# A four-layer network over eight batches on one core: normalized inputs made one stage earlier, a reciprocal spread over 64 rows, and new hand-written orders

## The reference

```python
x = x + _layernorm(_L0_attn_ref(_layernorm(x), ...))   # attention, 16 heads of 16, low-rank k and v, rotary part of 32, causal softmax
x = x + _layernorm(_L0_ffn_ref(_layernorm(x), ...))    # 256 -> 1024, relu squared, -> 256; ternary weights plus a rank-16 term
x = x + _layernorm(_L1_attn_ref(_layernorm(x), ...))   # the mixer, below
x = x + _layernorm(_L1_ffn_ref(_layernorm(x), ...))    # 256 -> 1024, relu, -> 256
```

```python
p_w = jnp.exp(log_p + log_tw)                 # 32 rows of 512
den = jnp.cumsum(p_w[..., 0], axis=1)
num_re = jnp.cumsum(pwb * jnp.cos(k_val[..., None] * theta), axis=1)
num_im = jnp.cumsum(pwb * jnp.sin(k_val[..., None] * theta), axis=1)
inv = lax.rsqrt(jnp.maximum(den, 0.0001)); inv = (inv * inv)[..., None, None]   # = 1 / max(den, 1e-4)
# sums of num * inv * query over 8 angles, then silu, then @ W_out
```

## Time and profile before

| what | us |
|---|---|
| median of 3 runs | 1694.96 (1694.31 to 1700.07) |
| profiled execution, its own time | 1691.56 |
| its span, first to last instruction | 1689.7 |
| busy: TensorE matmul / VectorE / ScalarE / GpSimd | 1298.3 / 1330.3 / 960.4 / 564.5 |

### The profile page before, as it was taken

One profiled execution on the slowest core, in us unless ns is written; L12 is line 12 of the kernel. 1 busy time (PEld: TensorE's weight loads), 2 busy tenths in 40 slices (PEclk: granted clock), 3 DMA queues, 4 the chain that ended last, 5 costly groups with the idle time before them and its releaser, 6 DMA issues.

```text
span 1689.7 us, 22269 instructions
## 1 busy us (share of the span) xinstructions
PE 1298.3 (77%) x7692; PEld 792.9 (47%) x7692; DVE 1330.3 (79%) x2794; ACT 960.4 (57%) x1637; POOL 564.5 (33%) x335
## 2 busy tenths in 40 slices
PE   4376886678779987988789988897799877865336
PEld 2244364435445554646455654564456455422214
DVE  4953347988788889987998899987989899778850
ACT  2165357744685578565865687457855794343301
POOL 1000301472054602570246314540546035505600
PEclk9589898779979998989899999999899989877668
DMA  5310223103311322131313131222203320012000
GB/s 181 75 38 1 63 45 100 59 24 83 87 60 38 75 65 88 38 87 38 95 57 77 31 100 59 68 52 63 96 25 75 71 82 26 13 61 78 13 0 13
DMA packets 62431, 101.38 MB, mean 60 GB/s; under 512 B 8192, under 2 KB 32144, under 8 KB 62320
## 3 DMA queue, kind: packets, MB, share of 16 engines
q1 hardware_dynamic: 62320, 99.95, 21.4%
HBM read 74.24 MB, written 25.69 MB: 59 GB/s over the span
## 4 chain that ended last, share of the span: by engine, by line
PE 33%; DVE 22%; ACT 12%; issue 12%; POOL 10%; DMA 8%; SPq 2%; POOLq 0%; DVEq 0%; ACTq 0%
PE ps L752 13%; PE ps L762 10%; POOL work L719 5%; DVE work L1304 4%; DVE work L1223 4%; DVE work L1313 3%; ACT work L1001 3%; DMA work<-weights 2%; ACT work L1008 2%; DVE norms L1134 2%; PE ps L833 2%; DMA work<-values 2%; POOL norms L687 2%; PE ps L815 2%; PE ps L890 2%
## 5 line engine op out<-in xcount | busy, mean ns | idle before, releaser
L719 POOL TENSOR_TENSOR work<-work 128x1024 f32<-128x1024 f32 x128 | 336.5, 2654 | 480.9 <-ACT work L1056 400.3
L1001 ACT ACTIVATE work<-work 128x384 f32<-128x384 f32 (+3 forms) x512 | 264.7, 558 | 168.7 <-DVE work L1223 167.8
L1304 DVE TENSOR_TENSOR_SCAN work<-ps,work 128x512 f32<-128x512 f32 x256 | 302.2, 1209 | 17.5 <-POOL work L719 17.0
L1223 DVE CUSTOM_DVE_ANT_0 work<-ps,work 128x384 f32<-128x384 f32 (+3 forms) x512 | 226.8, 485 | 109.1 <-PE ps L807 106.5
L815 PE MATMUL ps<-ident,work 128*128 128x128 f32 x1280 | 217.3, 298 | 53.8 <-DVE work L1223 44.5
L687 POOL TENSOR_TENSOR norms<-norms,power 128x4 f32<-128x4 f32 x64 | 71.3, 1114 | 498.8 <-DVE norms L1140 498.7
L815 PEld LDWEIGHTS ps<-ident,work 128*128 128x128 f32 x1280 | 160.1, 152 | 130.1 <-DVE work L1223 77.2
L1313 DVE TENSOR_TENSOR work<-work 128x1024 f32<-128x1024 f32 x128 | 215.2, 1681 | 5.1
L1008 ACT COPY work<-ps 128x512 f32<-128x512 f32 x320 | 181.2, 571 | 46.3 <-PE ps L815 46.2
L807 PE MATMUL ps<-work 96*128 96x384 bf16 (+3 forms) x512 | 132.5, 327 | 47.8 <-ACT work L1008 39.3
L752 PE MATMUL ps<-xTd,wf 128*128 128x512 f32 x256 | 126.0, 629 | 11.5 <-ACT xTd L966 7.9
(11 more groups left out here) (161 smaller groups left out, 1937.5 us busy)
## 6 DMA issues: line engine op xcount, KB each, us to landing
work<-values SPq DMA_DIRECT2D x64, 256.0 KB
work<-weights SPq DMA_DIRECT2D x64, 256.0 KB
scratch<-work SPq DMA_DIRECT2D x32, 384.0 KB, 5.1
work<-scratch SPq DMA_DIRECT2D x64, 192.0 KB, 3.7
work<-scratch SPq DMA_DIRECT2D x64, 128.0 KB, 4.0
x_in<-x SPq DMA_DIRECT2D x8, 512.0 KB, 3.4
work<-scratch SPq DMA_DIRECT2D x64, 64.0 KB, 4.0
weights<-work SPq DMA_DIRECT2D x8, 512.0 KB, 4.6
```

The costliest lines, as they stand in the source:

```text
L719: g_.tensor_tensor(wave, wave, pwr[:, slot, None, :].to_broadcast([P, MH, T]), ALU.mult).then_inc(*weighed[half].one)
L1001: i = s_.activation(part_of, part_of, ACT.Exp, scale=-1.0, bias=nmax[:, row:row + 1])
L1223: i = v_.tensor_tensor_reduce(sc[:, n % 4, at:at + nk], out_of(name)[:, at:at + nk], base_of(qt), -SCORE_SCALE, BIG, ALU.add, ALU.min, nma ...
L1304: v_.tensor_tensor_scan(ring[:, at, m, :], still.to_broadcast([P, T]), ring[:, at, m, :], 0.0, ALU.add, ALU.add).then_inc(*scanned.one)
```

## The change

Six edits come together.

1. The head of attention for batch b+1 (`stats`, the split-off `centre`, `norm`, `xT`) moves into the end of attention of batch b. `x_in` gets two buffers, SP loads x two stages ahead (`fetch`), the y statistics get a slot of `norms` and signals of their own.
2. The head of a first dense stage (`fstats`, `fnorm`, `fxT`, now `head_items`) moves ahead of `gproj` of the second dense stage that precedes it in chain `d`.
3. The reciprocal: DVE stores max(total, 1e-4) first, SP writes it to a new HBM tensor `totals`, loads it back as 64 rows of 256, DVE inverts that, SP writes `inverses`. Chain `m` has four `inv` items instead of two.
4. The preparation: only `wo`'s centring (3 DVE instructions, `means` 0) must be done before `out` of the first batch; it has become an item of its own. The rest is interleaved with the first batch's attention. In the first batch DVE takes the odd `T` copies over from ACT (`on_act`), 20 of 40.
5. `plan_banks` gives every use of a bank over the whole program a number, instead of a pattern per batch. The banks are the same groups.
6. The pieces of q are sent before those of k; all five tables of orders are written anew.

The core of the diff (`...` marks what is left out; of the tables one line stands):

```diff
 def attention_items(b):
-    items = ["stats", "norm", "xT", "ckv", ("q", 0), ("q", 1), "qr", ("k", 0), ("k", 1), "kr", "pieces", ("v", 0), ("v", 1),
-             ("base", 0), ("base", 1), ("base", 2), ("base", 3), ("group", 0), ("group", 1)]
+    items = ["ckv", ("q", 0), ("q", 1), ("pieces", 0), "qr", ("k", 0), ("k", 1), ("pieces", 1), "kr", ("v", 0), ("v", 1),
+             ("base", 0), ("base", 1), ("base", 2), ("base", 3), "fetch", ("group", 0), ("group", 1)]
+    after = b + 1 < B
...
-    return steps(b, items + ["attnT", "out", "ystats", "sum"])
+        if n == ALL - 4:
+            items += ["stats+", "centre+"] * after
+    items += ["attnT"] + ["norm+"] * after + ["out"] + ["xT+"] * after + ["ystats", "sum"]
+    return steps(b, items)
...
 def second_dense_items(b):
-    return steps(b, ["oout", "oystats", "osum", "gstats", "gnorm", "gxT"] + [("gc", g) for g in range(HC)] +
-                 [("gproj", 0), ("gproj", 1), "gystats", "gsum"])
+    return (steps(b, ["oout", "oystats", "osum", "gstats", "gnorm", "gxT"] + [("gc", g) for g in range(HC)]) + head_items(b + 2) +
+            steps(b, [("gproj", 0), ("gproj", 1), "gystats", "gsum"]))
+
+def head_items(b):
+    return steps(b, ["fstats", "fnorm", "fxT"]) if b < B else []
...
-             ("turn", 1), ("frac", 1), ("inv", 0), ("turn", 2), ("frac", 2), ("turn", 3), ("frac", 3)]
+             ("turn", 1), ("frac", 1), ("inv", 0), ("turn", 2), ("frac", 2), ("turn", 3), ("frac", 3), ("inv", 1)]
...
-        items += unit_items(u)
-    items += [("gather", 0), ("inv", 1)] + unit_items(4) + ...
+        items += unit_items(u) + [("inv", 2)] * (u == 1)
+    items += [("gather", 0), ("inv", 3)] + unit_items(4) + ...
...
-        "a5 p10 a3 p12 a90 d a15 d a4 d a4 d a18 d a5 d a4 d a4 d a4 m2 a4 m2 a3 m a4 m2 a4 m2 a2 m2 a2 m a2 "
+        "a p a9 p a2 p a5 p a4 p5 a4 p2 a5 p a p9 a2 p a4 p a62 d a24 d a4 d a2 d a10 d a3 d a6 d a4 d a4 m2 "
...
-def on_act(m):
-    return True
+def on_act(b, m):
+    return b > 0 or m % 2 == 0
...
                 if item == "out":
                     if b == 0:
-                        pe.wait_ge(prep_step, N_PREP)
+                        pe.wait_ge(prep_step, N_WO)
...
# SP
                 if item == "inv" and n == 0:
-                    need(sp, inv_ready, b, 1)
-                    sp.dma_start(inverses[b], total).then_inc(*tot_saved.one)
+                    need(sp, tot_ready, b, 1)
+                    sp.dma_start(totals[b], zs).then_inc(*tot_saved.one)
                 if item == "inv" and n == 1:
                     need(sp, tot_saved, b, 1)
+                    need(sp, inv_saved, b - 1, 1)
+                    sp.dma_start(spread, totals[b].rearrange("k (i t) -> (k i) t", i=2)).then_inc(*tot_loaded.one)
+                if item == "inv" and n == 2:
+                    need(sp, inv_ready, b, 1)
+                    sp.dma_start(inverses[b].rearrange("k (i t) -> (k i) t", i=2), spread).then_inc(*inv_saved.one)
+                if item == "inv" and n == 3:
+                    need(sp, inv_saved, b, 1)
...
# ACT
                 if item == "fnorm":
-                    need(act, g_sum, b - 2, 1)
+                    if b:
+                        is_filled(act, *((b - 2, "gxT1") if b > 1 else (0, "zxT1")))
...
# DVE
-                    step(inv_step, v_.tensor_tensor_scan(total, still[0:K].to_broadcast([K, T]), zs,
-                                                         0.0, ALU.add, ALU.add))
-                    step(inv_step, v_.tensor_scalar(total, total, 1e-4, None, ALU.max))
-                    v_.reciprocal(total, total).then_inc(*inv_ready.one)
+                    step(inv_step, v_.tensor_tensor_scan(zs, still[ZS:ZS + K].to_broadcast([K, T]), zs, 0.0, ALU.add, ALU.add))
+                    v_.tensor_scalar(zs, zs, 1e-4, None, ALU.max).then_inc(*tot_ready.one)
+                if item == "inv" and n == 1:
+                    need(dve, tot_loaded, b, 1)
+                    v_.reciprocal(spread, spread).then_inc(*inv_ready.one)
```

362 lines of the change are left out of this document (186 added, 176 removed), and 76 rows, old and new, of the table MERGE.

## The result

The changed kernel takes 1641.5 us (median of 4 runs, 1634.3 to 1644.4) against 1696.0 beside it, a ratio of 0.967 with a 95% interval of 0.963 to 0.971. A second set of 5 runs gave 1639.6, ratio 0.970 (0.968 to 0.972). The forecast was 1639. The profiled execution is the fastest of the first set: 1634.28 us, span 1632.2.

What follows compares the result with a forecast made beforehand. Waits bound the filling, nearly full VectorE and TensorE batches 3 to 7, then a run-down tail. Windows 158 + 167 + 162 + 872 + 275 = 1634, 1636 as execution time, plus 3.4 to the median: 1639 us, own range 1620 to 1652.

Steps and rivals of the forecast that it cites:

- it is 19 now, with the same steps in between: End of batch 0: from the last score to attention's `sum` stays 19 us, putting `sum` at 158.
- The 7 us for the head: Batch 1: attention's head made early takes 7 us off the 174.4 us window, bounds 0 and 24.
- I take 27 of the 39 off: Batches 3 to 7: early heads and kept mixer work remove 27 of VectorE's 39.0 us waits for TensorE's scores.
- 3 for each of the five, 15: Batches 3 to 7: VectorE's new wait for the reciprocal's store and load, 0 to 5.3 us, taken as 3 per batch.
- my sign of being wrong: Steady stages: a new long wait of VectorE or TensorE, most likely on the reciprocal's transfer, would show the prediction wrong.
- My upper bound of 900: Batches 3 to 7: longest expected time, with idle 118 us, each reciprocal wait at 5.3 and nothing won.
- half of 3.34: The reciprocal on 64 rows by 256 takes half of 3.34 us, 1.7 less, if time goes by elements per partition.
- A store at the median and a load at the least make 11.1: Reciprocal's round trip by HBM: 11.1 us, from earlier landings of 4.3 to 13.8, median 6.8.
- The slower rival: Each batch's reciprocal: its round trip blocks VectorE, up to 21.8 us per batch, total 1789 us; chance 0.06.
- Only the filling gains: Batches 3 to 7 stay at 888 or a bit over, both engines nearly full; total about 1660 us; chance 0.20.
- Only the work counts: Whole kernel: other waits refill each shortened wait, leaving only work changes and partly hidden preparation; about 1681 us; chance 0.08.
- Filling in full: Batch 1 gains 24 us, batch 2 starts its mixer early, steady idle falls to 63; about 1597 us; chance 0.18.

## Why the prediction was right, step by step

**The books.** The total is right to within 3 us. The filling and the deferred mixer work went much as forecast. In the steady stages the mechanism is right only in part: of the 23.1 us won there 14.2 are shorter work, where I had 3.9, and 8.9 are idle time, where I had 12. Two parts missed in opposite ways, batch 0 by +4.4 and batches 3 to 7 by -7.1, so that the total is closer than its parts by luck.

**Batch 0, 158 forecast, 162.4 measured.** The first score came at 48.5 where I said 55, but the last ended at 141.7, not 139: between 48.5 and 100 VectorE was busy 48.7 of 51.5 us:

```profile
48.50:100.00 51.50, 27.58 (x192) 18.03 (x192) 48.73 (x99) 18.43 (x35) 0.00 (x0) 0.63 0.10 22
```

The preparation was moved beside the scores, and it was not hidden, since the same engine does both. The step "it is 19 now, with the same steps in between" failed: from the last score's end to `sum`'s end it took 20.8. The reason stands in the windows of `attnT` and `out`, before and after, and in the projection's own rows (before, after):

```profile
159.30:165.00 5.70, 4.77 (x24) 3.81 (x24) 0.00 (x0) 1.07 (x2) 0.00 (x0) 1.00 0.00 0
```

```profile
148.90:157.40 8.50, 7.62 (x26) 6.16 (x27) 0.00 (x0) 2.77 (x6) 0.00 (x0) 0.60 0.00 0
```

```profile
161.32 3.69 PE L762 MATMUL ps<-wo,xTa 128*128 128x256 f32 x16 [0.93 <-ACT xTa L966]
```

```profile
151.54 5.85 PE L783 MATMUL ps<-wo,xTa 128*128 128x256 f32 x16 [0.88 <-ACT xTa L987]
```

The granted clock was 0.60 in that stretch, mostly the lower of its two levels (1.2 and 2.4 GHz), where it had been 1.00. The projection and the transposes took 2.9 us longer, of which 0.8 came back between the last score and the transposes. TensorE had been busy 10.7 of the 18.9 us ahead of it, at a granted clock of 1.00. The same 0.60 shows in this stretch with the old orders, where it takes 8.6 us, so it is not the new orders alone that bring it. Nor does the busy time ahead tell the cases apart: in the 18.9 us ahead of the stretch it was 11.9 us in the kernel before, which stayed at 1.00, and 12.0 with the old orders, which fell. Of all the traces only the kernel before and the one with the preparation first and the copies on ScalarE have the projection at 3.7 us; in the others it takes 5.2 to 6.0. What brings it is open.

**Batch 1, 167 forecast, 166.7 measured.** The 7 us for the head were a guess between 0 and 24, and that it was met so closely is luck. With the head late again the window is 6.9 us longer, so the head is the cause.

**Batch 2, 162 forecast, 162.5 measured.** VectorE's work is 133.2 against 131.4 in the sum, its idle time 29.3 against 31. The trace has 24 scans, 12 mixes and 6 `turn` and `frac` pairs in that window, 6, 3 and 2 fewer than before, as the order said.

**Batches 3 to 7, 872 forecast, 864.9 measured.** Idle time: 90 forecast, 93.4 measured, from two errors that cancel in part. The step "I take 27 of the 39 off" was too large: 15.9 went. The step "3 for each of the five, 15" was too large as well: the wait came once, 9.7 us, in batch 4. That is longer than the 5.3 that I had as the most, and a new long wait on this transfer was my sign of being wrong; it came in one batch of five. My upper bound of 900 was also added up wrongly: 102.2 and five times 5.3 are 129 of idle time, not 118, so the bound was 911. The work was the larger error: 781.9 forecast, 771.6 measured. It lies in a term that the sum did not have. The same instructions became shorter; `mix` and `frac` in this stretch, before and after (busy us, mean ns):

```profile
L1313 DVE TENSOR_TENSOR work<-work 128x1024 f32<-128x1024 f32 x78 | 126.0, 1615 | 3.0
L1297 DVE SCALAR_TENSOR_TENSOR work<-work,smalls 128x512 f32<-128x512 f32 x78 | 64.8, 872 | 1.0
```

```profile
L1338 DVE TENSOR_TENSOR work<-work 128x1024 f32<-128x1024 f32 x79 | 121.9, 1544 | 2.3
L1322 DVE SCALAR_TENSOR_TENSOR work<-work,smalls 128x512 f32<-128x512 f32 x80 | 61.2, 806 | 0.8
```

`mix` fell from 1615 to 1544 ns and `frac` from 872 to 806, together 11 us over the 79 and 80 instructions of the stretch. Not all of it is the order: with the old orders on the changed code they take 1580 and 812 there. But `turn` takes 722 ns then and 585 in the changed kernel, and the three together 236.4 us against 226.5. Two `mix` of batch 6 in VectorE's timeline of the kernel after, and GpSimd's products there in its own:

```profile
1339.91 1.23 DVE L1338 TENSOR_TENSOR work<-work 128x1024 f32<-128x1024 f32 x1
...
1345.00 3.28 DVE L1338 TENSOR_TENSOR work<-work 128x1024 f32<-128x1024 f32 x1
```

```profile
1342.50 10.29 POOL L740 TENSOR_TENSOR work<-work 128x1024 f32<-128x1024 f32 x4 [10.62 <-ACT work L1080]
```

The `mix` ahead of the products takes 1.23 us, the one beside them 3.28, so the same instruction is not always equally long, and an order also sets what it falls beside. That GpSimd is the cause is read from such overlaps and was not tried by itself.

**The reciprocal.** The step "half of 3.34" holds:

```profile
L1301 DVE RECIPROCAL work<-work 64x256 f32<-64x256 f32 x8 | 13.9, 1740 | 12.2 <-DMA work<-totals 12.1
```

**The round trip.** "A store at the median and a load at the least make 11.1": it is 9.0 and 2.1 in the medians above, the same sum by luck. The earlier trace rows hold the broadcast loads of 256 KB as well as the store; the store alone had landed in 6.0 to 9.0 us there. And what the transfer takes goes by what the queue was given just before: 1.6 and 2.1 us behind an idle queue, up to 9.5 and 2.1 behind the loads of weights. The cover is what I had too small in most batches and nearly right, at 5.8 us, in batch 4 (4.6), where the queue added 2.8 us. The Trainium skill ("DMA: Bandwidth & Descriptors", section "Anatomy of one DMA") has about 2 us and bytes by bandwidth for one transfer, as a fit to DMAs issued from GpSimd, where these are SyncE's. The load's 2.1 us and the three stores of 1.6 agree with that. By the page the uncovered reciprocal would have waited 4.3 us in each batch; it waited 3.8 or 3.9 in three of them and 10.8 to 14.5 in the five with loads just ahead.

**The slower rival.** I gave it 0.06 and a deciding point of 10 us per batch. With a wait of 9.5 us per batch the kernel took 1712, 0.9% slower than before, so the mechanism is real and the deciding point lies below that. My price for it, 1639 - 24 + 76 = 1691, was 21 us too low. What spared the changed kernel is the place of the reciprocal in the order alone.

**The other rivals.** "Only the filling gains" would need steady stages of 888; they took 864.9, and the late head gives 39.5 us of them back. That is more than the 23.1 won: with the head late the steady stages take 904.4, 16.4 more than in the kernel before. So the other new orders and the round trip cost time there unless the head is early. My sum had only 15 for that, and which of them costs was not tried. "Only the work counts" is ruled out by the same row. "Filling in full" failed at the dense chain: the first `turn` of batch 0 came at 253.6, still 91 us behind `sum`. Its price was also added up wrongly: from 90 to 63 us of idle time are 27, not 15, so its time was 1585.

**The tail, 275 forecast, 275.7 measured.** VectorE is idle 17.2 us up to the last `turn` (23.5 before) with 13.7 us more work in it. The wait for POOL went, and one of 11.9 for a gather came; taking that one away changed nothing.

**Left open.** How much of the gain is the early head of the feed-forward, and how much the deferred mixer work, wasn't tried apart. Of the 64.5 us of the orders, 45.5 hang on attention's head and some 6 on the start; these parts need not add.

## What to carry to other kernels

A chain of small steps at the head of a stage costs the whole delay that it brings, here 7 to 8 us in each batch, when the busiest engine stands in it, even in stages where two engines show 88 and 87%; start it a stage ahead and price it by the chain, and not by the waits under one name. A transfer there and back in the middle of the busiest engine's work needs cover for its whole length, the issuing queue included: here 14.4 us at worst, and the same edit ranged from -11 to +71 us by its place. Read what the queue was given just before the transfer, batch by batch: a median over all of them hides that the uncovered wait was 4 us or 11 to 15. Moving work beside other work of the same engine hides nothing; splitting what the second engine had to do ended the first batch 3.4 us earlier.

## What was not expected of the hardware

A 64 KB store from SBUF to HBM let its load follow after 1.6 us where SyncE had issued nothing for 17 us or more, and after 8.7 to 9.5 us directly behind four loads and a store of 256 KB each; the load back took 2.1 us. The granted clock of TensorE fell from 1.00 to 0.60 in the output projection of batch 0 in the changed kernel, 2.9 us for 24 matmuls. And one VectorE instruction, `mix`, had a mean of 1.54 us in the steady stages with the changed orders, 1.58 with the old orders on the same code and 1.62 in the kernel before; single ones took 1.23 and 3.28 us within 6 us of each other.
